# 32-head attention as one block without transfers: float32r parts in 32 rows per head, maxima turned in with the queries, keys made beside the feed-forward

## The reference, cut to what matters

```python
def _L1_xattn_ref(q, k, v):           # q = layernorm(x), k = v = ctx_512
    QH, KVH = (32, 8); D = E // QH; G = QH // KVH
    qh = q.reshape(b, s, KVH, G, D).transpose(0, 2, 3, 1, 4)
    kh = k.reshape(b, s, KVH, D).transpose(0, 2, 1, 3)
    vh = v.reshape(b, s, KVH, D).transpose(0, 2, 1, 3)
    scores = jnp.einsum('bkgsd,bktd->bkgst', qh, kh) / sqrt(8)
    attn = jax.nn.softmax(scores, axis=-1)
    return jnp.einsum('bkgst,bktd->bkgsd', attn, vh)   # heads side by side again
x = x + _L0_attn_ref(...); x = x + _L0_xattn_ref(...); x = x + _L0_ffn_ref(...)
x = x + _L1_attn_ref(...)
x = x + _L1_xattn_ref(_layernorm(x, axis=-1), ctx_512, ctx_512)
x = x + _L1_ffn_ref(...)
```

## Time and profile before

| what | us |
|---|---|
| three executions: median (lowest to highest) | 926.72 (925.44 to 932.48) |
| the profiled execution's own time | 928.2 |
| its span, first to last instruction | 926.4 |
| mean granted TensorE clock | 0.904 of full |
| ln5's first instruction to the first reduction of maxima | 662.11 to 692.85 |
| first to last reduction (128 of them) | 692.85 to 797.6 |
| last reduction to ln6's first instruction | 797.6 to 818.4 |

### The profile page before, as it was taken

The page is one execution under the profiler, slowest core; times in us unless marked ns, Lnnn a source line. Parts: engine busy times, 40 slices in busy tenths (PEclk is TensorE's granted clock), DMA queues, the critical chain, the costliest instruction groups (busy, mean ns, idle before and its releaser), DMA issues. The chain is left out here.

```text
span 926.4 us, 14056 instructions
## 1 busy us (share of the span) xinstructions
PE 750.6 (81%) x4790; PEld 480.8 (52%) x4818; DVE 592.6 (64%) x1130; ACT 422.7 (46%) x879; POOL 205.9 (22%) x312
## 2 busy tenths in 40 slices
PE   6999859999899998998362448999518999849998
PEld 3555555666566665665221323666403444348787
DVE  5579485565565655655765973575537999582766
ACT  4468533453634536345155325455224666522322
POOL 3322020311303113031303422230041111041441
PEclk9999989999999999999776558999856999977999
DMA  4534332020111201001210004152061111001211
GB/s 130 146 98 122 102 67 64 31 68 27 42 33 36 68 24 46 27 12 24 65 20 23 1 7 142 48 161 82 1 201 41 40 43 34 2 2 43 96 46 46
DMA packets 52357, 53.48 MB, mean 58 GB/s; under 512 B 11297, under 2 KB 41985, under 8 KB 52297
## 3 DMA queue, kind: packets, MB, share of 16 engines
q1 hardware_dynamic: 47772, 51.55, 19.4%
q10 hardware_dynamic: 4524, 1.14, 0.6%
HBM read 29.62 MB, written 5.09 MB: 37 GB/s over the span
## 5 line engine op out<-in xcount | busy, mean ns | idle before, releaser
L1189 DVE TENSOR_REDUCE x_nm<-ps 128x2 f32<-128x512 f32 x128 | 84.9, 686 | 23.8 <-PE ps L1257 21.8
L536 DVE TENSOR_REDUCE a_nm<-ps 128x2 f32<-128x512 f32 (+1 forms) x112 | 75.3, 688 | 30.5 <-PE ps L838 18.5
L1225 ACT ACTIVATE x_pt<-ps 128x1024 f32<-128x1024 f32 x64 | 62.1, 1021 | 33.3 <-PE ps L1294 33.3
L2011 PE MATMUL ps<-m_xp,m_mp 128*128 128x512 f32 x288 | 74.9, 401 | 1.7 <-DVE m_wr L1739 1.7
L1725 DVE TENSOR_TENSOR m_qcs<-ps,mw_tab 128x512 f32<-128x512 f32 x96 | 61.8, 686 | 22.1 <-PE ps L2011 21.2
L1888 ACT ACTIVATE m_junk<-ps,m_nm 128x256 bf16<-128x256 f32 x128 | 58.8, 485 | 36.8 <-DVE m_nm L1751 36.8
L681 ACT ACTIVATE a_pt<-ps 128x1024 f32<-128x1024 f32 x64 | 58.0, 916 | 32.2 <-PE ps L889 15.2
L1711 POOL TENSOR_SCALAR fw<-fw,finv 128x256 f32<-128x256 f32 x24 | 11.7, 487 | 255.0 <-PE ps L2091 255.0
L1257 PE MATMUL ps<-a_ks,a_qs 126*128 126x256 bf16 x256 | 53.3, 294 | 17.3 <-DMA a_ks<-scr_xk 15.8
L2011 PEld LDWEIGHTS ps<-m_xp,m_mp 128*128 128x128 f32 x288 | 52.2, 191 | 14.1 <-issue 4.5
L2820 PE MATMUL ps<-x_xp,x_wp 128*128 128x512 f32 x216 | 55.9, 410 | 2.6 <-DVE x_h3g L2742 2.6
(11 more groups left out here) (272 smaller groups left out, 1697.5 us busy)
## 6 DMA issues: line engine op xcount, KB each, us to landing
a_qs<-a_parts SPq DMA_DIRECT2D x48, 128.0 KB, 2.4
a_ks<-a_parts SPq DMA_DIRECT2D x48, 128.0 KB, 2.4
m_q<-m_qs SPq DMA_DIRECT2D x32, 128.0 KB, 2.2
x_gb<-scr_g SPq DMA_DIRECT2D x8, 512.0 KB, 3.6
fw<-in_f_w SPq DMA_DIRECT2D x12, 256.0 KB, 3.4
scr_xq<-xs_qp SPq DMA_DIRECT2D x12, 256.0 KB
a_qs<-scr_xq SPq DMA_DIRECT2D x32, 96.0 KB, 2.1
mw_wq<-in_m_wq SPq DMA_DIRECT2D x8, 256.0 KB, 2.9
```

Source lines behind the costliest of these rows:

```text
L536: dve.tensor_reduce(dst, src, AX.X, ALU.max, negate=True).then_inc(mx_done.sem, 1)
L1189: dve.tensor_reduce(dst, src, AX.X, ALU.max, negate=True).then_inc(mx_done.sem, 1)
L1225: act.activation(pt[:, i % 2, kt, 0:banks * BANK], c.ps[:, 2 + 2 * kt:2 + 2 * kt + banks, :].rearrange("p b n -> p (b n)"), ACT.Exp, scale ...
L2011: mm = pe.matmul(c.ps[:, QB_BANKS[k], :], mp[:, p % 2, w, dt, tile * P:(tile + 1) * P], xp[:, x, dt, half_cols(half)], start=((dt, w, x) = ...
```

## The change

- The four blocks of the 32-head attention become one, `cross_attention`, with no transfer but the 12 loads of experts' weights, which SyncE now issues at its start (they leave the attention of layer 1). The DRAM scratch and `split_context`, `attention_stage`, `normalise_stage` and the call of `layer_norm("ln5")` go.
- Queries and keys are float32r in two parts (high, low); each head has 32 rows of partitions: three products of 8 channels (24 rows), one row for the maximum, the rest unused. The 4 heads of a group fill 128 partitions. Queries are laid out by tokens in `q3` and turned by matmuls against a float32r identity (`turn_queries`, 16 chunks: 4 ahead of the loop, 12 in slots of it).
- VectorE's reduction writes the negated maxima straight into column 24 of each head in `q3`; `turn_maxima` turns queries and maxima together once more, and ScalarE copies them to `q2`, from which `scores_t` reads 25 rows. GpSimd's split and the transfer go.
- Scores run LAG = 3 items ahead, turned maxima TLAG = 2. 12 of the 16 half tiles of outputs are turned and divided in slots of the loop, 4 behind it; GpSimd adds them to x. From item 17 on ScalarE copies the outputs out instead of VectorE.
- VectorE and ScalarE prepare the first sequence (2 token tiles), GpSimd the other 6 tiles.
- `KeyRows`: the keys are split in the first block of the feed-forward (ScalarE, GpSimd) and turned in the second (TensorE: 256 float32 matmuls of 128 columns in column groups, two chunks of 16 ahead of each tile's transposes; ScalarE: two copies of 128x512 per tile).
- To make room, several buffers move into `c.fw` and `c.xnT`, and `junk` becomes bf16.

```diff
-def attention_block(c, st, name, wqk_in, wvo, bias_io, alibi=False, first=None, scales=None, late_loads=None, last_loads=None):
+def attention_block(c, st, name, wqk_in, wvo, bias_io, alibi=False, first=None, scales=None, last_loads=None, spare=None):
...
-        rest = sb("rest", [P, 2, BANK])
+        rest = (sb("rest", [P, 2 * BANK])[:, :] if spare is None else spare[:, 5 * FFN:6 * FFN])\
+            .rearrange("p (b n) -> p b n", b=2)
...
-        pt = (first.pt if first is not None else sb("pt", [P, 2 * QT * 4 * SEQ]))[:, :]\
+        pt = (first.pt[:, :] if first is not None else spare[:, 0:4 * FFN])\
...
-        wqk = sb("wqk", [P, 2, DT, DIM])
+        wqk = (sb("wqk", [P, 2 * DT * DIM])[:, :] if spare is None else spare[:, 4 * FFN:5 * FFN])\
+            .rearrange("p (w t o) -> p w t o", w=2, t=DT)
...
-def attention_stage(c, name, hd, shared_k, scale, v, scr_q, scr_k, av_all, alibi=False):
...
-def split_context(c, v):
...
-        xq = sb("xq", [P, TT, DIM], BF16)
-        xqT = sb("xqT", [P, DT, TOK], BF16)
+        xq = c.xnT[:, 0, :].bitcast(BF16).rearrange("p (t d) -> p t d", t=TT)
+        xqT = c.xnT[:, 1, :].bitcast(BF16).rearrange("p (t n) -> p t n", t=DT)
...
+                keys.load(sp)
...
+                keys.split_low(pool)
...
+                keys.split_high(act)
...
+                        for k in range(2 * t, 2 * t + 2):
+                            keys.copy(act, k)
...
+                            for k in range(2 * t, 2 * t + 2):
+                                keys.turn(pe, k)
...
+class KeyRows:
+    ROWS, GROUPS = 24, 8
...
+    def split_high(self, act):
+        act.activation(self.identr[:, :], self.c.ident[:, :], ACT.Copy).then_inc(self.high.sem, 1)
+        act.wait_ge(self.loaded.sem, 16)
+        for k in range(2):
+            act.activation(self.flat[:, :, 8 * k:8 * k + 8], self.heads, ACT.Copy).then_inc(self.high.sem, 1)
+    def split_low(self, pool):
+        pool.wait_ge(self.c.cleared.sem, self.c.cleared.at(1))
+        pool.memset(self.flat[:, :, self.ROWS:SCOLS].bitcast(F32), 1.0).then_inc(self.ones.sem, 1)
+        pool.wait_ge(self.high.sem, 3)
+        pool.wait_ge(self.ones.sem, 1)
+        pool.tensor_tensor(self.flat[:, :, 16:24], self.heads, self.flat[:, :, 0:8].bitcast(F32), ALU.subtract)\
+            .then_inc(self.low.sem, 1)
+    def turn(self, pe, k):
+        g, half = divmod(k, 2)
+        if k == 0:
+            pe.wait_ge(self.low.sem, 1)
+        if k >= 4:
+            pe.wait_ge(self.copied.sem, k - 3)
+        for j in range(TT // 2):
+            for h in range(4):
+                mm = pe.matmul(self.c.ps[SCOLS * h:SCOLS * (h + 1), 4 + k % 4, j * P:(j + 1) * P],
+                               self.flat[:, (half * TT // 2 + j) * self.GROUPS + g, :].bitcast(F32), self.c.ident[:, :],
+                               start=True, stop=True)
+        mm.then_inc(self.turned.sem, 1)
+    def copy(self, act, k):
+        g, half = divmod(k, 2)
+        act.wait_ge(self.turned.sem, k + 1)
+        act.activation(self.kT[:, g, half * BANK:(half + 1) * BANK], self.c.ps[:, 4 + k % 4, :], ACT.Copy)\
+            .then_inc(self.copied.sem, 1)
+def cross_attention(c, keys):
+    LAG, TLAG = 3, 2
+    EARLY = 2
+    CHUNKS = 2 * TT
+    TAIL = 12
+    SLOTS = {n: ("queries", k) for k, n in enumerate((2, 3, 4, 5, 6, 7, 8, 9, 13, 14, 15, 16), 4)}
+    SLOTS.update({n: ("outputs", s) for s, n in enumerate((10, 11, 12, 17, 18, 19, 20, 21, 24, 25, 26, 27))})
+    OWN_COPIES = 17
+    RING = 4
...
+                def maxima(n):
+                    b, g = place(n)
+                    for u in range(4):
+                        dve.wait_ge(s_done.sem, s_done.at(4 * n + u + 1))
+                        dve.tensor_reduce(q3[:, QT * b:QT * (b + 1), g, u, ROWS],
+                                          c.ps[:, u % 2, :].rearrange("p (t k) -> p t k", t=QT),
+                                          AX.X, ALU.max, negate=True).then_inc(mx_done.sem, 1)
+                def outputs(n):
+                    b, g = place(n)
+                    dve.wait_ge(av_done.sem, av_done.at(n + 1))
+                    dve.tensor_scalar(av[:, g, seq_cols(b)], c.ps[:, 6, 0:SEQ], 1.0, None, ALU.mult)\
+                        .then_inc(out_done.sem, 1)
+                def quotients(s):
+                    bank = c.ps[:, out_bank(s), :].rearrange("p (h s) -> p h s", s=SCOLS)
+                    dve.wait_ge(ot_done.sem, ot_done.at(s + 1))
+                    dve.reciprocal(rec[:, s % 2, :], bank[:, :, HD:HD + 1].squeeze(2)).then_inc(rec_done.sem, 1)
+                    dve.wait_ge(rec_done.sem, rec_done.at(s + 1))
...
+                    dve.tensor_tensor(on[:, s % 2, :, :], bank[:, :, 0:HD],
+                                      rec[:, s % 2, :].unsqueeze(2).broadcast_to([P, HEADS // 2, HD]), ALU.mult)\
+                        .then_inc(on_done.sem, 1)
+                statistics(0)
+                inverse(0)
+                for t in range(EARLY):
+                    normalised(t)
+                statistics(1)
+                for t in range(EARLY):
+                    low(t)
+                inverse(1)
+                for n in range(LAG):
+                    maxima(n)
+                for n in range(N):
+                    if n + LAG < N:
+                        maxima(n + LAG)
+                    if n < OWN_COPIES:
+                        outputs(n)
+                    if n in SLOTS and SLOTS[n][0] == "outputs":
+                        quotients(SLOTS[n][1])
...
+                for t in range(EARLY, TT):
+                    pool.tensor_scalar(c.xn[:, t, :], c.x[:, t, :], mv[:, t, 0:1], rstd[:, t:t + 1],
+                                       ALU.subtract, ALU.mult).then_inc(late_xn.sem, 1)
...
+                    for k in range(1, 4):
+                        pool.tensor_copy(columns(t)[:, :, k * HD:(k + 1) * HD], heads).then_inc(late_hi.sem, 1)
...
+                    pool.tensor_tensor(columns(t)[:, :, 0:HD], heads, columns(t)[:, :, HD:2 * HD].bitcast(F32),
+                                       ALU.subtract).then_inc(late_lo.sem, 1)
+                for s in range(16):
+                    t, half = divmod(s, 2)
+                    part = c.x[:, t, half * P:(half + 1) * P]
+                    pool.wait_ge(on_done.sem, on_done.at(s + 1))
+                    pool.tensor_tensor(part, on[:, s % 2, :, :].rearrange("p h d -> p (h d)"), part, ALU.add)\
+                        .then_inc(x_done.sem, 1)
...
+                def queries(k):
+                    b, j = divmod(k, 4)
+                    act.wait_ge(chunk_done.sem, chunk_done.at(k + 1))
...
+                    act.activation(qT[:, b % 2, 2 * j:2 * j + 2, :],
+                                   c.ps[:, chunk_bank(k), :].rearrange("p (g q) -> p g q", g=2), ACT.Copy)\
+                        .then_inc(chunk_ev.sem, 1)
+                def with_maxima(n):
+                    if n >= RING:
+                        act.wait_ge(st_done.sem, st_done.at(2 * (n - RING) + 2))
+                    act.wait_ge(tr_done.sem, tr_done.at(n + 1))
+                    act.activation(q2[:, n % RING, :], c.ps[:, 7, 0:SEQ], ACT.Copy).then_inc(q2_done.sem, 1)
+                def exponentials(n, pair):
+                    if n >= 2:
+                        act.wait_ge(av_done.sem, av_done.at(n - 1))
+                    act.wait_ge(st_done.sem, st_done.at(2 * n + pair + 1))
+                    act.activation(pt[:, n % 2, pair, :, :, :].rearrange("p h t q -> p (h t q)"),
+                                   c.ps[:, 2 + 2 * pair:4 + 2 * pair, :].rearrange("p b n -> p (b n)"),
+                                   ACT.Exp, scale=SCALE).then_inc(exp_done.sem, 1)
...
+                for n in range(N):
+                    if n + 1 < N:
+                        exponentials(n + 1, 0)
+                    if n + TLAG < N:
+                        with_maxima(n + TLAG)
+                    if n in SLOTS and SLOTS[n][0] == "queries":
+                        queries(SLOTS[n][1])
+                    if n + 1 < N:
+                        exponentials(n + 1, 1)
+                    if n >= OWN_COPIES:
+                        outputs(n)
...
+                def turn_queries(k):
+                    b, j = divmod(k, 4)
+                    if b == 0:
+                        pe.wait_ge(early_lo.sem, early_lo.at(EARLY))
+                    else:
+                        pe.wait_ge(late_lo.sem, late_lo.at(QT * b))
+                    for i in range(2):
+                        for qt in range(QT):
+                            mm = pe.matmul(c.ps[:, chunk_bank(k), i * SEQ + qt * P:i * SEQ + (qt + 1) * P],
+                                           q3[:, QT * b + qt, 2 * j + i, :, :].rearrange("p h s -> p (h s)"),
+                                           keys.identr[:, :], start=True, stop=True)
+                    mm.then_inc(chunk_done.sem, 1)
+                def scores(n, u):
+                    if n >= N:
```

(68 more changed lines are left out.)

640 lines of the change are left out of this document (201 added, 439 removed).

## The result

The changed kernel takes **990.49 us** (median of 4 runs, 987.65 to 991.09); beside it the kernel before took 929.6 (4 runs, 925.44 to 933.96). The ratio is 1.065, with an interval of 1.059 to 1.071: slower by 6.5%, where 914 was forecast and 897 to 935 given as the range.

A forecast was written before the change was run, and what follows sets the result against it. VectorE and TensorE were taken as nearly balanced in the attention's items, with uncomputed time ahead. Front -21.0, items +16.0, tail -9.1 and feed-forward +1.2 summed to -12.9 us: 914 us as a median, range 897 to 935.

The forecast's parts named there:

- TensorE, per item, at full clock: 32-head attention loop: TensorE's own work sums to 3.17 us an item, 3.74 with a slot, at full clock.
- rival D: Loop: matmuls of 24 rows, or stalls on the rings, leave TensorE at 1.2 GHz; 3.2 us more an item, about 1015; 0.04.
- Front: Attention's start to VectorE's first reduction: split, stores and reload go; first reduction at about 671.8 in place of 692.85, -21.0 us.
- rival A: Loop: row groups do not run side by side, turned scores cost 0.90, 0.45 more in 26 items; 926 us; chance 0.18.
- rival B: Loop: scores and turned scores overlap too, loads hide in changes, VectorE bounds at 3.3 an item; 899 us; chance 0.20.
- rival C: Loop: changes of the array's shape become the bound, 0.3 each instead of 0.125, 34.5 us more; 948 us; chance 0.11.
- Item at full clock: Loop: time per item with the lists' waits, 3.3 us without a slot, 3.87 with a query slot.
- The ring of copy and product: Loop, items 0 to 16: VectorE's output copy waits behind the product and precedes its next reduction; 3.3 us, 3.87 with query slot.
- the 80 us by which the loop missed: Loop, first to last reduction: forecast 120.7 us against 104.75 before, +16.0.
- Tail: Last reduction to ln6: items without maxima, last copy, transposes, divisions, addition; 11.7 us against 20.8, -9.1.
- Keys beside the feed-forward: Feed-forward: GpSimd's new work may cost the first block +1.2 us; second block taken as 0, bounds -6 and +10.
- The guess on the clock of the second block: Feed-forward's second block: with the keys' turning TensorE, half clocked before, should be granted full clock; 2.6 + 3.6 a tile fits.

The follow-up runs named there:

- the run with filling in eight items: Changed kernel plus six matmuls of 512 columns on the whole array, result overwritten, in each of items 0 to 7 and none after: 987.96 us, 1.064 of before.
- The kernel with all rows: Changed kernel with scores and turned scores reading all 128 rows, timing only, values wrong: 916.72 us, then 919.27, 0.987 of the kernel before.
- the run with six filling matmuls: Changed kernel plus six matmuls of 512 columns on the whole array, result overwritten, ahead of every item's turned maxima: 956.73 us.

## Why the prediction was wrong

**The step that failed** is the base of the whole item: "TensorE, per item, at full clock". It stood on the argument against rival D, "the present loop reaches 0.91 with its fill, and the list stays as dense". The list did stay dense, TensorE was busy 99% of the loop; but the scores of the kernel before read 126 rows, and both kinds of scores of the changed one 24 and 25, and the clock went with that: 0.50 in place of 0.91. With all rows read, and instructions, columns and waits as they were, it is 1.00 and an item 4.21 us in place of 6.73. Rival D named the mechanism, its second half ("or stalls on the rings") was wrong, and it got 0.04. Its price was 3.2 us an item; 6.73 against 4.11 is 2.6, so the time is 990 and not 1015.

The Trainium skill (TensorE: Matmul & The Clock Gate, Why this matters for your kernels) says that TensorE gets to the high clock by being kept busy without a break, and loses it in idle gaps. The trace does not agree for few rows: 199.3 of 200.8 us busy at 0.50, and a fall from 1.00 to 0.50 in the run with filling in eight items, with holes of 0.17 us at most ahead of it.

**The other steps, one by one.**

- *Front.* First reduction at 670.78, forecast 671.8. Right, part by part: the two subtractions end at 668.1, forecast 669.2, and 2.7 us pass from there to the first reduction, forecast 2.6.
- *Row groups side by side (rival A).* They overlap, in pairs almost at once, as taken, and scores run beside turned scores too, which only rival B had.
- *Changes of shape (rival C).* 0.18 each, with a share of a small matmul, where ten were added, and 0.09 each where two were taken away; not the bound.
- *Item at full clock.* 4.11 with a query slot against 3.87 forecast. The ring of copy and product is there as described (VectorE's copy stands between product and reductions, 0.42), but in the filled run whose reductions are shown above TensorE waits only 0.17 in it; its own list takes 3.94 where 3.74 was counted. The kernel with all rows, which pays A's 0.45 and saves changes, takes 132 us for the loop. So of the 80 us by which the loop missed (200.8 against 120.7), I estimate from this kernel that about 69 are the clock and about 11 would have been missed at full clock as well; from the items, 2.6 us each in 29, it is 76.
- *Tail.* 12.7 against 11.7, its first part still at the low clock (0.74 over it).
- *Keys beside the feed-forward.* The -0.3 hides four parts. The feed-forward starts 2.3 later in the changed kernel's trace (459.15 against 456.89), where nothing of the change has run but buffers that moved; among the 15 traces of kernels with that same part it starts anywhere from 453.4 to 461.5. Its first block takes 38.3 us instead of 37.1, the **+1.2** of the forecast. Its second block, where I took 0, takes 51.4 instead of 55.9, **-4.4**, within the bounds given (50.8 to 53.4 in the 15 traces). The attention of layer 1 takes 0.7 more. The guess on the clock of the second block was right: 0.82 instead of 0.50. The turning of the first tile's keys, at 0.50, takes 3.64 us (3.6 was counted); of a later tile's, at full clock, 1.95, and in the middle of the stage a tile comes every 4.60 us in place of 6.35 (517.48 to 522.08, before 517.09 to 523.44). Whether the clock or GpSimd's shifted product brings that was not tested.
- *Experts.* 104.6 after ln6's start instead of 108.0, not forecast. Before, the chain of waits shows transfers of the gates (0.5% and 0.4% of the span) that it doesn't show after; the cause was not looked for.

```profile
494.03:549.90 55.87, 23.29 (x128) 14.52 (x128) 44.30 (x74) 18.10 (x18) 20.72 (x8) 0.50 0.03 10
```

This line is the second block of the feed-forward in the kernel before, over its whole length; that of the changed kernel stands in the table above.

The kernel with all rows is 1.3% faster than before, where 1.4% was forecast for the plan. That the two agree is in part luck: its loop is 11 us longer than forecast, but what lies before the attention took 4.3 less than forecast (659.0 in place of 662.1, with 1.2 more expected) and the experts 3.7 less.

## What to carry to other kernels

Before packing small matmuls into row groups, ask what the clock of TensorE will see: in this kernel the same list at 24 of 128 rows ran at half the clock for 200 us with TensorE 99% busy, and reading all 128 rows, most of them against zeros, made the kernel 6 to 7% faster. A busy share of 100% doesn't say at which clock; read the granted clock of each stage, and in a forecast ask of each new stage whether its matmuls use the array as the old one's did. If a layout leaves rows empty, a block diagonal operand made by an idle engine can cost less than the lost clock, and one operand may serve several uses. It has to reach enough of the matmuls: on the turned scores alone it left the clock at 0.50 and made the kernel slower still (1060).

## What the runs showed of the hardware

- In this loop the granted clock went with the rows that the scores read, and not with how long TensorE was busy: 0.50 with all 16 matmuls of scores of an item on 24 or 25 rows; 1.00 behind the first 10 us with all 16 on 128 rows, zeros among them or not (behind the first 26 with small matmuls of few rows between them); with eight of 16 on all rows either 0.50 for 91 us and then 1.00 (the scores) or 0.50 throughout (the turned scores).
- Six full matmuls of 512 columns an item beside the unchanged row groups brought it to 1.00 as well, two did not.
- TensorE need not be busy all the time for the full clock: in the second block of the feed-forward, where float32 matmuls of 128 rows into 32 columns were added, it is 1.00 with TensorE busy 7.77 of 10 us.

```profile
520.00:530.00 10.00, 7.77 (x187) 6.28 (x188) 9.35 (x18) 6.87 (x10) 4.72 (x2) 1.00 0.01 2
```

- The way up and the way down seem to differ: two filling matmuls an item never reached the high clock from below, and kept it for 38 us from above, in one run each.
- Not shown: whether it is the number of rows or the addressing by row groups that counts. Every matmul of few rows here is also one of a row group, and no run kept all four row groups busy at once. The edits also changed the rows of both operands together.
- Row groups of different heads overlap across instructions of different kinds. At full clock, in the run with six filling matmuls, four scores and four turned scores of 256 columns take 0.68 us (771.66 to 772.34) with a change of shape, where eight in a row at 0.11 would take 0.88:

```profile
771.66 0.38 PE L2389 MATMUL ps<-kr_kT,x_qT 24*128 24x256 f32 x1
771.67 0.38 PE L2427 MATMUL ps<-x_q,kr_kT 25*128 25x256 f32 x1
771.88 0.28 PE L2389 MATMUL ps<-kr_kT,x_qT 24*128 24x256 f32 x1
771.89 0.38 PE L2427 MATMUL ps<-x_q,kr_kT 25*128 25x256 f32 x2
...
772.34 1.65 PE L2407 MATMUL ps<-kr_kT,kr_ident 128*128 128x512 f32 x6
```
